# Layer 1 attention: q and k projected already transposed, with rotary halves exchanged by DMA

## The reference

```python
x = x + attn0(layernorm(x))        # 16 heads of 16, low-rank parts, alibi, causal
x = x + ffn0(layernorm(x))         # 8 experts, one chosen per token
x = x + attn1(layernorm(x))
x = x + ffn1(layernorm(x))         # fp4 quantised, 704 wide
# attn1, the block that the change touches
proj = x @ W_in.T + b_in           # 256 -> 3 * 16 * 64
q, k, v = heads(proj)              # each (8, 16, 512, 64)
q, k = rope(q), rope(k)            # y_lo = x_lo*cos + x_hi*sin ; y_hi = x_hi*cos - x_lo*sin, halves of 32
att = softmax(causal(q @ k.T / 8))
y = (att @ v) @ W_out.T + b_out
```

## Time and profile before

| | us |
|---|---|
| runs: median (lowest, highest) of 3 | 2312.48 (2310.83, 2312.55) |
| the profiled execution's own time | 2315.66 |
| its span, first to last instruction | 2313.9 |
| TensorE busy in the span | 1965.5 (85%) |
| VectorE | 1723.1 (74%) |
| ScalarE | 1398.9 (60%) |
| GpSimd | 1036.8 (45%) |
| transposes of x for sequence 0 of layer 1 begin | 949.2 |
| first scores of layer 1 | 1000.6 |
| last output projection of layer 1 starts its last product | 2001.4 |

### The profile page before, as it was taken

How to read it: one execution, slowest core, us unless ns; L and a number is a source line. 1 busy time by engine, 2 the same in 40 slices (tenths; PEclk the granted TensorE clock), 3 DMA queues, 4 the chain that set the end, 5 groups by cost and what they waited for, 6 DMA issues and landing times. The chain is left out here.

```text
span 2313.9 us, 52728 instructions
## 1 busy us (share of the span) xinstructions
PE 1965.5 (85%) x18758; PEld 1405.2 (61%) x18759; DVE 1723.1 (74%) x3717; ACT 1398.9 (60%) x2736; POOL 1036.8 (45%) x1231
## 2 busy tenths in 40 slices
PE   2889989899862999378799999999999999549999
PEld 1666666666561666145577777676767777426665
DVE  4778888788791444468678787879696977679997
ACT  1666666666562444267668696868787878344443
POOL 4435534355014000488747576657575663132222
PEclk9999999999955999689999999999999999869999
DMA  7000000000033332002100000000000000100000
GB/s 241 2 1 2 2 2 2 2 2 2 3 128 127 98 91 79 12 11 35 22 1 2 2 2 2 2 1 2 1 2 2 2 2 2 38 1 14 18 18 23
DMA packets 53114, 57.77 MB, mean 25 GB/s; under 512 B 7121, under 2 KB 47217, under 8 KB 52897
## 3 DMA queue, kind: packets, MB, share of 16 engines
q1 hardware_dynamic: 46240, 45.00, 6.2%
q0 software_dynamic: 6656, 9.85, 2.0%
HBM read 36.22 MB, written 18.61 MB: 24 GB/s over the span
## 5 line engine op out<-in xcount | busy, mean ns | idle before, releaser
L371 PE MATMUL a_bank<-w_in_sb,xnT_sb 128*128 128x512 f16 x1152 | 293.7, 394 | 33.7 <-DVE t_buf_sb L579 26.4
L1116 DVE TENSOR_REDUCE neg_max_sb<-a_bank 128x1 f32<-128x128 f32 (+3 forms) x512 | 236.1, 485 | 92.6 <-PE a_bank L896 88.7
L531 DVE TENSOR_REDUCE neg_max_sb<-a_bank 128x1 f32<-128x128 f32 (+3 forms) x512 | 236.1, 482 | 92.6 <-PE a_bank L288 91.1
L1039 ACT ACTIVATE probT_sb<-a_bank 128x512 f32<-128x512 f32 (+1 forms) x384 | 198.8, 526 | 145.3 <-PE a_bank L919 140.5
L442 ACT ACTIVATE p_hi_sb<-a_bank 128x384 f16<-128x384 f32 (+1 forms) x384 | 205.3, 535 | 120.7 <-PE a_bank L297 119.0
L434 ACT ACTIVATE prob_sb<-a_bank,neg_max_sb 128x128 f32<-128x128 f32 (+3 forms) x512 | 261.4, 543 | 23.9 <-DVE neg_max_sb L531 23.0
L538 DVE TENSOR_TENSOR p_lo_sb<-a_bank,p_hi_sb 128x384 f16<-128x384 f32 (+1 forms) x384 | 228.0, 595 | 59.7 <-ACT p_hi_sb L442 56.1
L453 ACT ACTIVATE stack_sb<-a_bank 128x1024 f16<-128x1024 f16 (+1 forms) x256 | 211.4, 826 | 7.0 <-PE a_bank L342 6.6
L297 PE MATMUL a_bank<-ident_f_sb,prob_sb 128*128 128x128 f32 x1280 | 206.4, 276 | 3.7 <-DVE p_lo_sb L538 3.1
L707 POOL TENSOR_TENSOR rope_w_sb<-t_buf_sb,sin_sb 128x256 f32<-128x256 f32 x128 | 146.0, 1140 | 134.7 <-DVE t_buf_sb L579 132.2
L371 PEld LDWEIGHTS a_bank<-w_in_sb,xnT_sb 128*128 128x128 f16 x1152 | 104.9, 100 | 143.0 <-DVE t_buf_sb L579 34.2
(11 more groups left out here) (268 smaller groups left out, 5613.3 us busy)
## 6 DMA issues: line engine op xcount, KB each, us to landing
sorted_rows<-zeros_sb SPq DMA_DIRECT2D x1, 4992.0 KB, 21.6
x_in_sb<-sorted_rows SPq DMA_DIRECT2D x39, 128.0 KB, 2.1
sorted_results<-y_moe_sb SPq DMA_DIRECT2D x39, 128.0 KB, 1.7
x_sb_sb<-L_attn_x SPq DMA_DIRECT2D x8, 512.0 KB, 10.7
w_raw_sb<-L_ffn_gate_bank SPq DMA_DIRECT2D x8, 512.0 KB, 3.6
w_raw_sb<-L_ffn_up_bank SPq DMA_DIRECT2D x8, 512.0 KB, 4.7
w_raw_sb<-L_ffn_down_bank SPq DMA_DIRECT2D x8, 512.0 KB, 5.8
out<-x_sb_sb SPq DMA_DIRECT2D x32, 128.0 KB, 1.7
```

The lines of the kernel that those rows point to most:

```text
L371: last = pe.matmul(out, xnT[:, x, c, j * P:(j + 1) * P], w["in"][:, w_, c, cols], start=k == 0, stop=k == len(terms) - 1)
L531: last = dve.tensor_reduce(neg_max[:, i:i + 1], S[(3 * h + g) % 2][:, off:off + L], AX.X, ALU.max, negate=True)
L1039: act.activation(probT[:, (h // 4) % 2, h % 4, T_AT[r]:T_AT[r + 1]], ST[(3 * h + r) % 2][:, 0:T_AT[r + 1] - T_AT[r]], ACT.Exp).then_inc(s_ ...
L1116: last = dve.tensor_reduce(neg_max[:, h % 2, i:i + 1], S[(3 * h + g) % 2][:, off:off + L], AX.X, ALU.max, negate=True)
```

## The change

`attention` is taken out (layer 0 did not use it) and `attention1` written for layer 1:

- **q and k come out of the projection transposed.** The weights of two heads (128 columns) are now the stationary operand and the 512 tokens the moving one, so a unit (t, p), t for q or k and p for one of 8 pairs of heads, is again six matmuls of 512 columns and has head dimensions on the partitions. The stack with its transposes and copies is gone, and q_stage and k_stage. 16 units per sequence take the place of 16 pieces; v keeps its 8 pieces.
- **The exchange of halves** is by DMA: ScalarE copies a unit with bias to `t_buf`; when q and k of a pair are there, the sync engine issues four transfers of 32 partitions (q and k side by side, 4 KB each) that swap the halves into `t_sw`. VectorE adds the bias and multiplies by the cosines from the work bank in one instruction; GpSimd multiplies `t_sw` by the sines and adds; ScalarE and GpSimd make high and low part (z_hi, z_lo). In a slot ScalarE's order is: rounding of v, `rope_hi`, p_hi, copies out of the work banks, exponentials.
- **Scores** are three products over the 64 rows of the head (rows 0 to 63 of the pair's tile for even heads, 64 to 127 for odd ones).
- **The output projection** takes yT in two 16-bit parts and the output weights in two: 24 matmuls of 256 columns per tile. The low part of yT is a VectorE instruction more; the output weights are loaded at the stage's start (1 MB) and split by ScalarE and VectorE ahead of slot 0.
- **Slots.** q units at slots 1, 7, ... and k units at 3, 9, ... (those of the first two pairs in the sequence before, or ahead of slot 0), v at 5, 11, 14, 17 and 29, 32, 35, 41. Ahead of slot 0 stand 4 units and 4 v pieces. xnT has two buffers.
- Tables of sines, cosines and biases change shape; layer 0's semaphores are cleared and freed after its block, with one barrier.

```diff
-    LAG_T, LAG_HI, LAG_LO, LAG_PV, LAG_WA, LAG_WV = LAGS[layer]
...
+    LAG_T, LAG_HI, LAG_LO, LAG_PV = 2, 2, 3, 4
+    LAG_WA, LAG_WV, LAG_VH, LAG_VL = 0, 1, 3, 4
+    LAG_W, LAG_ZH, LAG_ZL = (5, 4), (6, 5), (7, 6)
...
-                    q = stack[:, h % 2, i * P:(i + 1) * P]
-                    pe.matmul(out, q, stack[:, h % 2, T:T + L], start=True, stop=False)
-                    pe.matmul(out, q, stack[:, h % 2, 2 * T:2 * T + L], start=False, stop=False)
+                rows, at_q, at_k = slice((h % 2) * DH, (h % 2 + 1) * DH), 2 * (pr % 2), 2 * (pr % 2) + 1
+                for n, (q, k) in enumerate(((z_hi, z_hi), (z_hi, z_lo), (z_lo, z_hi))):
+                    pe.matmul(out, q[rows, at_q, i * P:(i + 1) * P], k[rows, at_k, 0:L], start=n == 0, stop=False)
                 last = pe.matmul(out[:, L - P:L], ident_b[:, :], mask[:, :], start=False, stop=True)
...
+                wait(pe, s_xnT, (b + 1) * QT)
+                for n, (x, w_, c) in enumerate(terms):
+                    last = pe.matmul(out, w["in"][:, w_, c, t * 1024 + p * P:t * 1024 + (p + 1) * P], xnT[:, b % 2, x, c, :],
+                                     start=n == 0, stop=n == len(terms) - 1)
...
+                wait(act, s_fill, n)
+                wait(act, s_sw, 16 * 4 * (unit(b, t, p) // 2))
+                act.activation(t_buf[:, t, :], W[bank][:, :], ACT.Identity, scale=1.0 / W1_SCALE,
+                               bias=w["bias_qk"][:, 0, t * PAIRS + p:t * PAIRS + p + 1]).then_inc(s_t, 1)
+        def rope_hi(b, t, p):
+            wait(act, s_z, U + 1)
+            wait(act, s_scores, 6 * (U // 2 - 1))
+            act.activation(z_hi[:, U % 4, :], rope[:, U % 4, :], ACT.Copy).then_inc(s_zh, 1)
...
+                wait(dve, s_t, U + 1)
+                wait(dve, s_zl, U - 3)
+                dve.scalar_tensor_tensor(out=rope[:, U % 4, :], in0=W[bank][:, :],
+                                         scalar=w["bias_qk"][:, 1, t * PAIRS + p:t * PAIRS + p + 1],
+                                         in1=w["cos"][:, t, :], op0=ALU.add, op1=ALU.mult).then_inc(s_u, 1)
...
+            wait(pool, s_sw, 16 * 4 * (U // 2 + 1))
+            pool.tensor_tensor(t_sw[:, t, :], t_sw[:, t, :], w["sin"][:, t, :], ALU.mult).then_inc(s_w, 1)
+            wait(pool, s_u, U + 1)
+            wait(pool, s_w, U + 1)
+            pool.tensor_tensor(rope[:, U % 4, :], rope[:, U % 4, :], t_sw[:, t, :], ALU.add).then_inc(s_z, 1)
...
+    @block.sync
+    def _(sp):
+        sp.dma_start(out_raw, d["w_out1"].rearrange("(c p) n -> p c n", p=P)).then_inc(s_raw, 16)
+        for pr in range(B * PAIRS):
+            wait(sp, s_t, 2 * pr + 2)
+            wait(sp, s_z, 2 * pr)
+            for r in range(0, P, 32):
+                src = r + 32 if r % 64 == 0 else r - 32
+                sp.dma_start(t_sw[r:r + 32, :, :], t_buf[src:src + 32, :, :]).then_inc(s_sw, 16)
...
+            nc.clear_and_free_semaphores(a0_sems)
+            nc.all_engine_barrier()
```

More of the change, by code:

```diff
@@ L52 @@
 AT0 = ((1, 4, 7, 10), (13, 16, 19, 22), (24, 27, 30, 33), (31, 34, 37, 40), (17, 20, 23), 24, 26, (63, 66), (73, 76, 91, 94))
[L53 to L62, removed]
+AT1 = (tuple(6 * p - 11 for p in range(HEADS // 2)), tuple(6 * p - 9 for p in range(HEADS // 2)),
+       (5, 11, 14, 17), (29, 32, 35, 41), (20, 23, 26, 28), (55, 56, 57, 58), 1)
 class Tally:
@@ L1296, in load_columns @@
         sp.dma_start(self.w_raw[:, :, cols], d["w_in1"].rearrange("(c p) n -> p c n", p=P)[:, :, cols]).then_inc(self.s_raw, 16)
[L1297 removed]
+        m = HEADS * DH1 // of
+        sp.dma_start(self.bias[:, bass.ds(i * m, m)],
+                     d["L1_attn_b_in"][bass.ds(i * m + 2 * HEADS * DH1, m)].unsqueeze(0).to_broadcast([P, m])).then_inc(self.s_bias, 16)
     def load_rest(self, sp, d, part):
[L1301 to L1303 removed]
+        rest = []
         if part == 0:
[L1305 removed]
+            rest = [(self.bias_out[:, :], d["L1_attn_b_out"].unsqueeze(0).to_broadcast([P, D])),
+                    (self.bias_qk[:, 0, :], d["b_qk1"])]
         if part > 1:
             t = part - 2
[L1308 to L1309 removed]
+            rest = [(dst[:, t, :], src[t]) for dst, src in ((self.cos, d["cos"]), (self.sin, d["sin"]))]
         for dst, src in rest:
@@ L1420, in l1_attention @@
     with nc.Block() as block:
-        attention(block, 1, x_sb, stats, consts,
-                  {"in": w_in, "out": l1.w_out, "bias": bias, "bias_out": l1.bias_out, "cos": l1.cos, "sin": l1.sin},
-                  lambda n: sem(n + "_a1"), psb, banks, (act_aside, dve_aside, pool_aside))
+        attention1(block, x_sb, stats, consts,
+                   {"in": w_in, "bias": bias, "bias_qk": l1.bias_qk, "bias_out": l1.bias_out, "cos": l1.cos, "sin": l1.sin}, d,
+                   lambda n: sem(n + "_a1"), psb, banks, (act_aside, dve_aside, pool_aside))
 def load_expert(sp, d, w_raw, s_raw, e):
@@ L2377, in host_constants @@
     ss = np.concatenate([-sin, sin], -1).astype(np.float32)
-    c["cos"] = np.stack([cc * np.float32(0.125), cc])
-    c["sin"] = np.stack([ss * np.float32(0.125), ss])
+    rows = lambda m, s: np.tile((m * np.float32(s)).T, (P // DH1, 1))
+    c["cos"] = np.stack([rows(cc, 0.125 / W1_SCALE), rows(cc, 1.0 / W1_SCALE)])
+    c["sin"] = np.stack([rows(ss, 0.125), rows(ss, 1.0)])
     return c
```

1005 lines of the change are left out of this document (416 added, 589 removed).

## The result

The changed kernel takes 2359.4 us (median of 4 runs, 2358.0 to 2364.6) against 2312.5 of the kernel before on the same chip: ratio 1.0206, 95% interval 1.0187 to 1.0225. The forecast was 2332 in a range of 2298 to 2376. The direction and the range held; the step is +47 us where +20 was forecast, more than twice as much.

The account below looks back on a forecast made before the run. TensorE was taken to bound the middle sequences. 64 + 5 - 21 - 4 - 15 - 11.5 + 2 = +20 us on the profiled 2315.7 gave 2335, with the median 3.2 lower: 2332 us, range 2298 to 2376.

Parts of the forecast that it names:

- (a) to (d): TensorE's queue: third score product +69 us, row-mode changes +107.5, stack's transposes gone -84.5, output projection in 16 bits -28.
- the price of a switch: TensorE going between 128-row and 64-row products around the scores: 0.105 us each time, eight times a head.
- the output tile: Output projection on TensorE: 24 16-bit products taking 2.63 us a tile instead of 3.51, -28 us over 32 tiles.
- the 10.6 us ahead of the first row maximum: Start of the stage, before the first scores: first row maximum at 991 us instead of 1001.6.
- the first sequence's net: First sequence of layer 1's attention, bound by GpSimd: 15 of some 26 us of gaps given back, net +1.5 us.
- (e): Projections of q, k and v on TensorE: four formerly ahead of the first scores now run inside the sequences, +5 us.
- The stalls before (...) therefore shrink: TensorE's waits for work banks, exponentials and x transposes: shrink by 21 us in six middle sequences, 4 in the last.
- I cost them at nothing inside a sequence: Changed work of ScalarE, VectorE and GpSimd: all lighter than TensorE, so adding no time within a sequence.
- Cost nothing, with that margin: Exchange of halves by DMA: rotated q ready before ScalarE's rounding, cover 0.4 us plus 1, so no added time.
- my rival: Exchange arrives late at ScalarE's rounding of q: 1.2 us on 60 pairs, +70 us, 2402 in all; chance 0.10.
- that rival's number: Drained TensorE granted the lower clock more often: 0.97 in seven sequences, 2355 us in all; chance 0.12.

Follow-up runs that it names:

- exchange by unit: Changed kernel with x transposes at slots 23, 28, 29, 35 and q's and k's halves exchanged separately, each after its own bias: 2313.7 us, 1.0022 to before.
- high parts padded: Changed kernel, x transposes at 23, 28, 29, 35, high parts of q and k beside zero rows so scores run over 128 rows: 2272.2 us, 0.9833 to before.
- idle placing: Changed kernel with only the next sequence's x transposes moved to slots 23, 28, 29, 35, where GpSimd is idle during layer norms: 2326.2 us, 1.0048 to before.
- all three: Changed kernel with x transposes at 23, 28, 29, 35, q and k exchanged separately, and their high parts beside zero rows: 2256.2 us, 0.9779 to before.
- all 128 rows: Changed kernel with score products over all 128 rows of a pair, leaving out the separation of its two heads: 2301.8 us, 0.9952 to before.

## Why the prediction was wrong in size

- Right: (a) to (d) as TensorE's own work, the price of a switch (0.092 and 0.096 us, 0.10 with what follows; 0.105 taken), the output tile, the 10.6 us ahead of the first row maximum, and the first sequence's net +0.4 (+1.5 by my steps). (e) was not measured by itself.
- Failed: "The stalls before (...) therefore shrink: I give back 3.5 of 7.7 us in each of six middle sequences, -21, and 4 in the last, -4". The stalls of the work banks and exponentials did shrink, but I had counted the transposes of x among those that would, "now spread wider", and took for granted that nothing took their place ("I cost them at nothing inside a sequence"). Their wait for the layer norm grew from 1.0 to 17.8 us in the six sequences, and the clock fell behind it, for which the sum had nothing. I had read VectorE's load as a sum and never asked what its instructions stand beside once GpSimd's rotation falls elsewhere: GpSimd had less to do (406 us instead of 464 in the six sequences) and hit the layer norm more often. By my estimate the 43 us of these sequences are 44 of TensorE's own work (48 forecast) and 12 for 25 us more at the lower level (none forecast), less 13 that the waits gave back (21 forecast, and 13 only by difference). With the layer norm moved, they are 28 us shorter, more than their surplus of 16.
- In the last sequence no layer norm is left to make; there 14 us at the lower clock follow a wait of 1.1 us for an exponential. Half of that time is lost, some 7 of the 12 us over the forecast. It is gone in the kernel with the exchange by unit.
- Failed in part: "Cost nothing, with that margin" for the exchange. The lateness is near that of my rival, 0.95 us at 57 pairs inside the sequences where it had 1.2 at 60 (0.65 in the middle ones), but its price of 70 us is not there: middle sequences absorb it, and making it earlier gave 6.7 us in the last and 2.6 ahead of the first row maximum. The Trainium skill, DMA: Bandwidth & Descriptors, Rules for kernel authors, says that transfers to disjoint partitions serialize; the runs leave open whether that made the lateness, since the two exchanges differ in when they start.
- The clock: 0.97 for the six sequences was that rival's number, but the cause was not the drains (1.00 with all of them in the kernel before, 0.97 with none in the changed one). In the changed kernel it fell behind the waits for the layer norm. What tells a wait that costs the clock from one that does not is open, and so is why the clock stayed up in the kernel without exchange.
- Both repairs together bring the changed kernel to 1.0022 of the kernel before (1.0006 to 1.0037). What then keeps it from being faster is the switches, net 50 to 59 us: 50 by high parts padded against the idle placing (0.9833 and 1.0048, of two groups), 56 by all three against the exchange by unit (0.9779 and 1.0022, of one group), 59 by all 128 rows.

## What to carry to other kernels

Before moving work on GpSimd or VectorE, look in the timeline at what stands beside what: the layer norm's VectorE instructions, which read and write SBUF only, took 2.6 to 4.8 times as long beside GpSimd's, and a few slots' difference in a hand-written order was worth 84 us here (1.0048 to 1.0410) with the same instructions. A cost on the busiest engine has two prices, its own and the net one after waits; measure the second by putting that cost alone into the kernel before. And where a cheaper operand layout makes the array change its row mode, zeros that keep the mode may be cheaper than the smaller product.

## What the runs showed that I had not expected

- The give-back works both ways: taking 103 us of switches away doubled TensorE's waits, from 20.9 to 41.6 us in five sequences.
- A sequence with no wait in its records exists: the last one of the kernel with the exchange by unit, 108.90 us long, has TensorE busy for 108.90.
- On the sync queue it mattered here what a transfer waits for and what it stands behind, more than how many there are: 128 more of 128 KB, after the low parts and behind the next exchange, cost TensorE 102 us of waits; 256 more of 64 KB, after the high parts and ahead of it, none.
